# Products of weights and values for two batch entries per step, a fourth slot for transposed weights, and first loads in stages

## What is computed

```python
q, k, v = split_heads(ln(x) @ Wq.T + bq), split_heads(ctx @ Wk.T + bk), split_heads(ctx @ Wv.T + bv)
scores = einsum('bhqd,bhkd->bhqk', q, k) * NORM
scores = scores + where(mask == 0, -1e9, scores)      # layer 0 only
attn = softmax(scores, axis=-1)                       # 32 queries x 257 keys, 16 heads
ctx_out = einsum('bhqk,bhkd->bhqd', attn, v)          # the products of weights and values
x = x + ctx_out.transpose(0, 2, 1, 3).reshape(b, s, 128) @ Wo.T + bo
# then x = x + self_attention(ln(x)); x = x + experts(ln(x)); and the same again with layer 1's weights
```

## Time and profile before

| | us |
|---|---|
| median of three runs | 1146.7 |
| lowest, highest | 1142.59, 1146.88 |
| the profiled execution | 1144.7 |
| its span, first to last instruction | 1142.9 |
| TensorE busy (95% of the span) | 1083.9 |
| VectorE busy (73%) | 838.9 |
| ScalarE busy (64%) | 725.8 |
| GpSimd busy (45%) | 511.4 |
| mean granted clock of TensorE | 0.988 |

### The profile page before, as it was taken

One profiled execution on the slowest core, in us unless ns is written; L12 is line 12 of the kernel. 1 busy time (PEld: TensorE's weight loads), 2 busy tenths in 40 slices (PEclk: granted clock), 3 DMA queues, 4 the chain that ended last, 5 costly groups with the idle time before them and its releaser, 6 DMA issues.

```text
span 1142.9 us, 34921 instructions
## 1 busy us (share of the span) xinstructions
PE 1083.9 (95%) x13032; PEld 908.6 (80%) x13032; DVE 838.9 (73%) x2865; ACT 725.8 (64%) x2305; POOL 511.4 (45%) x712
## 2 busy tenths in 40 slices
PE   7798899999999999999999999999999999999898
PEld 5477787788877978887878878788788788887698
DVE  4455977687878866867868688686878757877785
ACT  6682478765676495667575775747657766556742
POOL 5386234435654345355444445354453354343430
PEclk9897999999999999999999999999999999999999
DMA  9520000000010000010000001010000000000000
GB/s 291 193 60 18 2 2 2 25 17 15 20 57 2 5 23 6 21 41 23 22 5 20 5 23 41 13 31 4 23 2 22 2 5 2 5 1 2 2 2 8
DMA packets 17748, 30.33 MB, mean 27 GB/s; under 512 B 2216, under 2 KB 14640, under 8 KB 16944
## 3 DMA queue, kind: packets, MB, share of 16 engines
q1 hardware_dynamic: 15280, 27.06, 7.8%
q10 hardware_dynamic: 2304, 1.05, 0.3%
HBM read 27.05 MB, written 1.05 MB: 25 GB/s over the span
## 4 chain that ended last, share of the span: by engine, by line
PE 61%; DVE 20%; ACT 9%; issue 5%; POOL 4%; DMA 2%; SPq 0%; DVEq 0%; ACTq 0%; POOLq 0%
PE bank L999 12%; PE bank L991 11%; PE bank L878 7%; PE bank L871 5%; PE bank L890 4%; PE bank L845 3%; PE bank L838 3%; PE bank L957 3%; ACT P L1039 3%; PE bank L976 2%; ACT PT L1050 2%; DVE P L1329 2%; DVE P L1319 2%; DMA maskb<-mask_in 2%; DVE xs L1339 2%
## 5 line engine op out<-in xcount | busy, mean ns | idle before, releaser
L991 PE MATMUL bank<-xnT,w 128*128 128x128 f32 x2048 | 259.4, 279 | 5.1 <-DVE P L1322 2.6
L991 PEld LDWEIGHTS bank<-xnT,w 128*128 128x128 f32 x2048 | 242.1, 193 | 11.7 <-issue 3.8
L1050 ACT COPY PT<-bank 128x512 f32<-128x512 f32 x256 | 149.9, 592 | 30.9 <-PE bank L878 29.1
L878 PE MATMUL bank<-cst,P 128*128 128x128 f32 x1024 | 153.8, 279 | 10.7 <-DVE nmax L1187 8.4
L878 PEld LDWEIGHTS bank<-cst,P 128*128 128x128 f32 x1024 | 114.3, 142 | 34.6 <-issue 14.5
L1042 ACT ACTIVATE P<-bank,nmax 128x257 f32<-128x257 f32 x256 | 123.2, 491 | 27.5 <-DVE nmax L1191 26.8
L1039 ACT ACTIVATE P<-P,nmax 128x257 f32<-128x257 f32 x256 | 131.7, 517 | 13.7 <-DVE nmax L1187 13.1
L999 PE MATMUL bank<-w2b,P 128*128 128x128 f32 x1024 | 130.8, 278 | 0.0
L1187 DVE CUSTOM_DVE_ANT_0 P<-bank,maskb,mscale 128x257 f32<-128x257 f32 x256 | 114.0, 481 | 20.9 <-PE bank L871 20.6
L999 PEld LDWEIGHTS bank<-w2b,P 128*128 128x128 f32 x1024 | 121.0, 192 | 5.7 <-issue 4.5
L1191 DVE TENSOR_REDUCE nmax<-bank 128x1 f32<-128x257 f32 x256 | 96.5, 413 | 39.1 <-PE bank L871 38.8
(11 more groups left out here) (133 smaller groups left out, 2198.4 us busy)
## 6 DMA issues: line engine op xcount, KB each, us to landing
ctxT<-ctx_in SPq DMA_DIRECT2D x16, 514.0 KB, 3.7
maskb<-mask_in SPq DMA_DIRECT2D x64, 128.5 KB, 2.8
w<-w_in SPq DMA_DIRECT2D x2, 2048.0 KB, 17.9
w2b<-w2b_in SPq DMA_DIRECT2D x1, 2048.0 KB, 26.1
wsq<-wsq_in SPq DMA_DIRECT2D x1, 1032.0 KB
xin<-x_in SPq DMA_DIRECT2D x16, 64.0 KB, 1.9
w2a<-w2a_in SPq DMA_DIRECT2D x1, 1024.0 KB, 17.2
out<-xs ACTq DMA_DIRECT2D x16, 64.0 KB, 1.5
```

The lines of the kernel that those rows point to most:

```text
L878: ins = nc.tensor.transpose(ps[:, k * 128:k * 128 + 128], P[s][:, 2 * m + k // 2, (k % 2) * 128:(k % 2) * 128 + 128], ident)
L991: ins = nc.tensor.matmul(ps[:, k * 128:k * 128 + 128], wt[:, m, k * 128:k * 128 + 128], xnT[s][:, :], start=True, stop=True)
L1050: nc.scalar.copy(PT[:, place, m % 2 * 512:m % 2 * 512 + 512], ps[:, :]).then_inc(pt_done[s], 1)
```

## The change

A `pv` step covers two batch entries (PAIRS = 2 to a group and layer): it waits for the four `ptrans` copies of both and issues 16 matmuls in a row. The slots of `PT` go from 3 to 4, and a `pv` gives back two. The scheduler's duration of a `pv` goes from 0.475 to 0.935. Its fitted numbers are all replaced, and so the order of all lists. SP's first loads are issued in stages, with six waits on landings.

```diff
-PTS = 3
+PTS = 4
+PAIRS = GB // 2
-        "ptrans": ((PE, 4 * TR + .03), (VACT, .47)), "pv": ((PE, .475),),
+        "ptrans": ((PE, 4 * TR + .03), (VACT, .47)), "pv": ((PE, .935),),
-FIRST = {("kproj", PE): (4.8, 9.7, 13.6), ("ln", DVE): (5.2, 10.0, 13.9), ("xpb", POOL): (5.2, 10.0, 13.9),
-         ("mask", POOL): (7.9, 11.8, 19.5), ("bo", PE): (20.5,), ("up", PE): (30.0, 30.0, 30.0)}
+FIRST = {("kproj", PE): (5.8, 9.5, 13.0), ("ln", DVE): (5.8, 9.5, 13.0), ("xpb", POOL): (5.8, 9.5, 13.0),
+         ("mask", POOL): (9.5, 13.0, 20.0), ("bo", PE): (18.0,), ("up", PE): (32.0, 32.0, 32.0)}
...
-            add("pv", l, b, ("ptrans", l, 2 * b + 1, VACT), *([] if b else [("vproj", l, 1, VACT)]))
+            if b % 2:
+                add("pv", l, b // 2, ("ptrans", l, 2 * b + 1, VACT), *([] if b > 1 else [("vproj", l, 1, VACT)]))
...
-STICK = 0.421
-EAGER, REACH, LAG = 0.1333, 0.001, 32.81
+STICK = 1.190
+EAGER, REACH, LAG = 0.3097, 0.000, 23.07
...
-            for s in range(STREAMS):
-                load_ctx(0, s)
-                load_x(0, s)
-                if s == 0:
-                    sp.dma_start(cst[:, :], const_d).then_inc(constants_in, 16)
...
-                load_mask(0, s)
-            for dst, src, loaded in ((w13[:, :, :], w13_d, experts0_in), (w2a[:, :, :, :], w2a_d, experts0_in),
-                                     (w1[:, :, :], w1_d, experts1_in), (w2b[:, :, :, :], w2b_d, experts1_in)):
-                sp.dma_start(dst, src).then_inc(loaded, 16)
+            load_ctx(0, 0)
+            load_x(0, 0)
+            sp.dma_start(cst[:, :], const_d).then_inc(constants_in, 16)
+
+            sp.wait_ge(ctx_in[0], 16)
+            load_mask(0, 0)
+            load_ctx(0, 1)
+            load_x(0, 1)
+            sp.wait_ge(mask_in[0], 64)
+            load_mask(0, 1)
+            load_ctx(0, 2)
+            load_x(0, 2)
+            sp.wait_ge(ctx_in[1], 16)
+            for dst, src in ((wsq[:, WFIRST:WSQ], wsq_d[:, WFIRST:WSQ]), (rows_in, brow_d[:, 0:512]),
+                             (router[:, :], brow_d[:, 512:520]), (b2[:, :], b2_d)):
+                sp.dma_start(dst, src).then_inc(others_in, 16)
+            sp.wait_ge(mask_in[1], 64)
+            load_mask(0, 2)
+            sp.wait_ge(others_in, 16 * OTHER_LOADS)
+            for dst, src in ((w13[:, :, :], w13_d), (w2a[:, :, :, :], w2a_d)):
+                sp.dma_start(dst, src).then_inc(experts0_in, 16)
+            sp.wait_ge(experts0_in, 16 * EXPERT_LOADS)
+            for dst, src in ((w1[:, :, :], w1_d), (w2b[:, :, :, :], w2b_d)):
+                sp.dma_start(dst, src).then_inc(experts1_in, 16)
...
-                    pe.wait_ge(pt_done[s], at(i, l, U // 2, 2 * m + 2))
+                    pe.wait_ge(pt_done[s], at(i, l, U // 2, 4 * m + 4))
...
-                    for k in range(2):
-                        for g in range(NGR):
...
+                    for b in (2 * m, 2 * m + 1):
+                        for k in range(2):
+                            for g in range(NGR):
...
-                        act.wait_ge(pv_done[hs], at(hi, hl, GB, hb + 1))
+                        act.wait_ge(pv_done[hs], at(hi, hl, PAIRS, hb // 2 + 1))
```

## The result

The changed kernel takes 1152.88 us (median; 1149.73 to 1155.45) beside 1145.26 for the kernel before on the same chip: ratio 1.0067, 95% interval 1.0051 to 1.0084. It is 7.6 us slower. I had forecast 1135, so the direction was wrong and the time lies above my range.

A forecast was written before the change was run, and what follows sets the result against it. TensorE's own stream was taken to set the pace. From the profiled 1144.7 us, -14.6 (visits) + 1.5 (pair waits) + 3 (staged loads) + 0 (new order) gave 1134.6, rounded to 1135; range 1123 to 1150.

The forecast's parts named there:

- The visits: On TensorE, 61 fewer entries into the pv matmul form, at 0.24 us each, save 14.6 us (9 to 21).
- Does it reach the end? I let it count in full: The 14.6 us saved on TensorE shorten the whole kernel in full, as TensorE waits only 34 us after 150 us.
- What the pair costs: TensorE's pv waits for four copies instead of two: +1.5 us taken, bounds nothing to 38 us.
- Rival C: TensorE waits before pairs for the fourth copy, 0.75 us each; over 1152.4 us from 26 of 64 steps; chance 0.14.
- The weights: New scheduler numbers reorder all steps: 0 us taken, bounds 11 us less to 11 us more.
- My ratio argument: In the scheduler, changing form costs 3.9 us of priority before and 4.2 after, so no fewer switches of other kinds.
- The stages: Six waits in SP's first loads delay the second-turn mask of stream 0: +3 us taken, bounds -8 to +9.
- Rival B: At the start, all SP waits cost, +9 us, and the clock stays down, 3 us more: 1144 us; chance 0.24.
- The signs: Wrong foundation if TensorE's waits after 150 us rise from 34 us by over ten, or other tiled visits increase.
- The stall itself: TensorE's 8.4 us wait near 41 us, behind a mask landing late after 7 MB of expert weights, is an order defect.

The follow-up runs named there:

- the crossed runs: Scheduler numbers swapped, loads at once: the kernel before with the changed kernel's numbers took 1248.7 us, the changed kernel with the old numbers 1213.3 us.

## Why the prediction was wrong

**The visits.** Priced rightly and counted nearly rightly: the traces have 123 visits before and 64 after (I had 125 and 64), and 607 form changes and 515. Splitting the pairs again cost more than I had priced, not less.

**"Does it reach the end? I let it count in full": this step failed.** It is the term of -14.6 us. With loads at once pairs and new order are worth nothing: 1145.1 us beside 1145.1, with an interval of about 2 us either way. I took a share of 97% busy from 150 us on as proof that TensorE's stream sets the time, with 34 us of waits as all that could stand against it. The runs show a slope for one direction only. Added work of 28 us costs 19 to 21, two thirds to three quarters; some 45 us taken away give nothing that the interval shows. The reading that fits is that many waits lie just below the surface of such a list, and a high busy share doesn't tell how deep. It is a reading: the late steps were counted, but not taken away one by one. My rows held a warning that I didn't use: ScalarE idles 30.9 us in front of the copies, 29.1 of it for TensorE's transposes, and with pairs in the old order these wait 5.3 us for ScalarE's exponentials. That is a ring, not a single file behind one engine.

**The clock, which I gave no term here.** I took TensorE's work at the clock that it had. But two kernels with less work in TensorE's list were granted less of it: 0.981 with loads at once, 0.976 with the even pv left out, against 0.985 to 0.986 before. Over the span that is 5 and 10.6 us of full clock less. Of the 74 executions of the kernel before in the sessions above, 29 had 0.987 and took 1144.2 us in the mean, five had 0.982 and took 1147.6, so 5.7 us of clock went with 3.4 us of time; in the kernel with the even pv left out it went one to one. By these two rates, as an estimate, 3 to 5 us of what pairs and new order should have saved are in the clock, 5 to 8 of the changed kernel's distance to the one before, stages included, and 6 to 11 of the 44 us. No run changed the clock alone, so whether it takes the time or only goes with the waits isn't shown.

**What the pair costs.** I had priced waits in front of pv at +1.5 us, and pv itself waits 0.4 us in all. What pairs lose in the old order, more than the whole of what they save (+11 to 13 us in the end), is elsewhere in the list: at transposes and scores and, it may be, in the clock. Rival C named a size that is not far from this (over 1152.4, against 1158.5) but put it at the wrong place, the fourth copy; the slots, too, never held a copy back.

**The weights.** "Taken: 0" with bounds of 11 us was right only in sum with pairs: the new order wins back the 11 to 13 us that pairs cost in the old one. My ratio argument, that staying in a form is worth 3.9 and then 4.2 us, held for the number of form changes. It said nothing of the order's worth, which ranges over 100 us by the crossed runs.

**The stages.** The mechanism was right, its size was off: +3 us taken, 7.3 to 7.8 measured, near my upper bound of 9. I let masks and context blocks cover four of six waits. In fact the DMA engines stand without transfers for 8.6 us in 40, most of it from 20 us on: the others' landing had to be waited for (issued from 14.67, landed 8.54 us later) and then the first half of the experts (10.64 us). The rule of the Trainium skill (DMA: Bandwidth & Descriptors, Rules for kernel authors: issue early, wait late) agrees with these runs. Rival B carried it. Its start, 9 us for the waits and 3 for the clock, was right in kind (the clock did stay down longer, 0.78 from 100 to 150 us) and dearer than the 7.3 to 7.8 measured; its 1144 is too low all the same, because the 14.6 us were not there.

**The signs.** Neither of the two that I had named for a wrong foundation came. TensorE's waits after 150 us rose from 34 to 36 us, not by ten, and the visits of other tiled steps went from 213 to 215. The signs looked at idle time alone, and what was lost lay before 150 us, below modelled ends and perhaps in the clock.

The stall itself was read rightly as a defect of the order of loads, and is the one thing that pays when mended.

## What to carry to other kernels

Where each engine follows a fixed list, the busy share of the busiest one is no bound that a saving can be subtracted from. Leave the work out once and see what comes back, before pricing an edit; padding alone would have misled here, since it costs where removal gives nothing. Read the granted clock beside each time: a kernel that waits more may also run slower. In a queue that keeps its order, put what is needed late behind what is needed soon, look at the next small load and not only at the one that stalls, and don't reach the same end by waits, which leave the transfers idle.

## What the runs showed of the hardware

A switch of TensorE's matmul form showed a steady price from start to start, after 150 us in the kernel before. An eight-record whole-array block took 0.893 us among its like, 0.987 where a tiled block followed and 0.995 behind a tiled one. Four transposes took 0.437, 0.530 and 0.493. The pv itself took 0.574 us, but 0.460 as the first half of a double, whose second half took 0.551 (1.01 in all).

With no masks behind them the constants land 3.8 us after their issue and not 5.1, and the first context block as before (3.8 and 3.7 us).

The clock is granted low not only behind the long wait: from 100 to 150 us it was 0.78 in the kernel after, where TensorE was busy 43.2 of 50 us, and 0.94 before, at 46.2. These are mixtures of its two levels, 2.4 and 1.2 GHz. Beside the stretch behind the long wait, the kernel after has the lower one from 95 to 115 and from 133 to 139 us, and the kernel before from 89 to 95 and from 99 to 105. In these stretches TensorE was busy 21.9 us at the lower level after the change and 10.5 before it.
